# Causal scores of a two-attention kernel: from four stages of 128x32 array tiles to two stages of 32x32 array tiles

## The reference, cut to what matters

```python
hn = layernorm(x, ln1_w, ln1_b)
qkv = hn @ in_proj_w.T + in_proj_b
q, k, v = ...                        # (s=32, b=256, 16 heads, 8)
scores = jnp.einsum('sbnd,tbnd->bnst', q, k) / np.sqrt(HEAD_DIM)
scores = jnp.where(causal[None, None], scores, -jnp.inf)
probs = jax.nn.softmax(scores, axis=-1)
attn = jnp.einsum('bnst,tbnd->sbnd', probs, v).reshape(s, b, h)
attn = attn @ out_proj_w.T + out_proj_b
x1 = x + attn
hn2 = layernorm(x1, ln2_w, ln2_b)
... router, top 2 of 8, gates ...
hmid = jax.nn.gelu(jnp.einsum('th,ehf->tef', hn2, w1), approximate=False)
y = jnp.einsum('tef,efh->th', hmid * gates[:, :, None], w2)
return x1 + y
```

## Time and profile before

| what | value |
|---|---|
| time, median of 3 runs | 1313.66 us (1312.94 to 1315.72) |
| span of the profiled execution | 1312.0 us, mean granted PE clock 0.982 of full |
| PE / PEld busy | 1219.3 us (93%) / 783.7 us (60%) |
| DVE / ACT / POOL busy | 1059.6 us (81%) / 960.6 us (73%) / 312.5 us (24%) |
| chain that ended last, by engine | PE 62%, ACT 18%, issue 9%, DVE 8% |
| first phase | 0 to about 653 us |
| second phase | 653 to 1312 us, a step every 39.5 us |

### The profile page before, as it was taken

One profiled execution on the slowest core, in us unless ns is written; L12 is line 12 of the kernel. 1 busy time (PEld: TensorE's weight loads), 2 busy tenths in 40 slices (PEclk: granted clock), 3 DMA queues, 4 the chain that ended last, 5 costly groups with the idle time before them and its releaser, 6 DMA issues.

```text
span 1312.0 us, 35299 instructions
## 1 busy us (share of the span) xinstructions
PE 1219.3 (93%) x12100; PEld 783.7 (60%) x12100; DVE 1059.6 (81%) x3074; ACT 960.6 (73%) x1696; POOL 312.5 (24%) x510
## 2 busy tenths in 40 slices
PE   2699999999999999999768999999999999999998
PEld 1456666555656566565335666676666676666676
DVE  5888888888888888888457887888887888887873
ACT  1388898888888898888756667776667776667744
POOL 4334433343333433341120111110111110111000
PEclk9899999999999999999869999999999999999999
DMA  3000000000000000000010000000000000000000
GB/s 94 5 15 15 14 17 17 17 13 13 17 17 13 13 17 17 17 14 15 17 29 17 26 10 17 24 24 24 24 8 16 24 24 24 24 4 20 17 10 16
DMA packets 50855, 24.93 MB, mean 19 GB/s; under 512 B 6384, under 2 KB 50288, under 8 KB 50800
## 3 DMA queue, kind: packets, MB, share of 16 engines
q1 hardware_dynamic: 50800, 24.21, 6.6%
HBM read 15.28 MB, written 8.39 MB: 18 GB/s over the span
## 4 chain that ended last, share of the span: by engine, by line
PE 62%; ACT 18%; issue 9%; DVE 8%; ACTq 1%; DMA 1%; SPq 1%; POOL 1%; DVEq 0%; POOLq 0%
PE bank L515 54%; ACT Kexp L1353 6%; PE bank L546 4%; ACT hmid L1438 4%; ACT prob L1331 3%; DVE smax L1002 2%; PE bank L596 2%; ACT prob L1364 1%; DVE prob L1006 1%; ACT KT L1322 1%; PE bank L615 1%; DMA x_in<-in_L_attn_x 1%; ACT oT L1272 1%; ACT feat L1286 1%; DVE Vexp L994 1%
## 5 line engine op out<-in xcount | busy, mean ns | idle before, releaser
L924 DVE TENSOR_REDUCE rowmax<-bank 128x2 f32<-128x512 f32 x512 | 336.7, 685 | 59.5 <-PE bank L515 56.3
L1331 ACT ACTIVATE prob<-bank 128x512 f32<-128x512 f32 x512 | 294.0, 601 | 29.2 <-PE bank L515 24.6
L515 PEld LDWEIGHTS bank<-w_sb,hmid 128*128 128x128 f32 x2048 | 244.0, 192 | 23.7 <-issue 11.7
L1438 ACT ACTIVATE hmid<-bank,up_scale 128x512 f32<-128x512 f32 x256 | 176.2, 733 | 110.1 <-PE bank L515 109.9
L515 PE MATMUL bank<-w_sb,hmid 128*128 128x128 f32 x2048 | 248.2, 276 | 0.0
L1353 ACT ACTIVATE Kexp<-bank,head_bias,head_mask 128x512 f32<-128x512 f32 x256 | 188.2, 848 | 42.5 <-PE bank L515 42.5
L515 PE MATMUL bank<-QT,KT 128*128 128x256 bf16 x1024 | 197.3, 275 | 10.2 <-ACT prob L1331 7.1
L515 PE MATMUL bank<-KT,QT 128*128 128x256 bf16 x1024 | 200.4, 279 | 5.7 <-DVE rowmax L924 5.1
L1222 DVE SCALAR_TENSOR_TENSOR acc<-bank,gate,acc 128x128 f32<-128x128 f32 x512 | 143.3, 342 | 72.3 <-PE bank L515 70.2
L515 PE MATMUL bank<-prob,V 128*9 128x256 f32 x2048 | 159.6, 384 | 0.0
L1322 ACT COPY KT<-bank 64x1024 bf16<-64x1024 bf16 x128 | 128.8, 1007 | 27.6 <-PE bank L546 23.1
(11 more groups left out here) (164 smaller groups left out, 1846.6 us busy)
## 6 DMA issues: line engine op xcount, KB each, us to landing
x_in<-in_L_attn_x SPq DMA_DIRECT2D x32, 128.0 KB, 2.1
QT<-shiftT SPq DMA_DIRECT2D x256, 2.0 KB
z_scratch<-z_out SPq DMA_DIRECT2D x32, 128.0 KB, 1.8
xg<-in_L_attn_x SPq DMA_DIRECT2D x64, 64.0 KB, 1.9
zg<-z_scratch SPq DMA_DIRECT2D x64, 64.0 KB, 2.0
out<-acc SPq DMA_DIRECT2D x64, 64.0 KB, 1.7
w_sb<-in_L_ffn_w SPq DMA_DIRECT2D x1, 1024.0 KB, 6.8
in_wT<-in_L_ffn_in_proj_w SPq DMA_DIRECT2D x1, 192.0 KB, 2.4
```

Of the source, the lines that this page charges most:

```text
L515: return pe.matmul(o, l, r, start=start, stop=stop, skip_group_check=True)
L924: dve.tensor_reduce(rowmax[h // 8][:, :, h % 2, h % 8 // 2], row_scores[h % 3][:].rearrange("p (s t) -> p s t", s=ST), AX.X, ALU.max).then ...
L1331: act.activation(prob[:, h % 8].rearrange("p t s -> p (t s)"), col_scores[h % 2][:], ACT.Exp, scale=1.0 / D).then_inc(s_exp, 1)
L1438: act.activation(hmid[e % 2][c][:], up_bank[c][:], ACT.Gelu, scale=up_scale[:, 0:1]).then_inc(s_mid, 1)
```

## The change

It does five things.

1. `Kexp` holds four copies instead of sixteen. Copy j keeps in each block of 32 features (four heads) only head j of that block (`quad_mask`), so one block's rows of the four copies hold four heads. ACT issues 4 instead of 16 activations per group; each still writes 128 x 512.
2. The scores matmuls contract 32 features instead of 128, in the row block r of the array, with 128 columns instead of 512. A bank now holds four heads of all four token tiles, instead of all heads of one tile. There are 64 such matmuls per group where there were 16.
3. The four banks' worth of results are made in two stages k, each with both banks: two causal matmuls (now in different row blocks) and 32 small ones. Stage 1 waits for `s_sdiff >= 4n + 2`, that is, until DVE has finished both results of stage 0.
4. `causal` and `seq_eye` are copied by DVE to the other three blocks of 32 partitions once, in `prepare`.
5. The tables place the pieces anew: on PE v at u=8 (was 12) and the stages at u=10 and 12 (the four tiles were at 14, 14, 15, 15); on DVE v at 9 (was 11) and the maxima at 10, 11, 12, 13 (were all at 14).

```diff
-PE_G = dict(hn=0, q=2, k=4, v=12, pv=4, scores0=14, scores1=14, scores2=15, scores3=15, merge=6, out=9,
+PE_G = dict(hn=0, q=2, k=4, v=8, pv=4, scores0=10, scores1=12, merge=6, out=9,
...
-            def causal_scores(n, t):
-                if t < 2:
-                    if positive(2 * (n - 1) + t + 1):
-                        pe.wait_ge(s_son, 2 * (n - 1) + t + 1)
-                else:
-                    pe.wait_ge(s_sdiff, 4 * n + t - 1)
-                m = score_bank(n, t)
-                mm(m[:], seq_eye[:].rearrange("k n s -> k (n s)"), causal[:].rearrange("k h t -> k (h t)"),
-                   stop=False)
-                for q in range(QUAD):
-                    c = t * P + q * SEQ
-                    ins = mm(m[q * SEQ:(q + 1) * SEQ, :], gqT[:, c:c + SEQ],
-                             Kexp[:, t * QUAD + q].rearrange("p h t -> p (h t)"), start=False)
-                ins.then_inc(s_sc, 1)
+            def causal_scores(n, k):
+                if k == 0:
+                    pe.wait_ge(s_kexp, n + 1)
+                    if positive(2 * n):
+                        pe.wait_ge(s_son, 2 * n)
+                else:
+                    pe.wait_ge(s_sdiff, 4 * n + 2)
+                for r in (2 * k, 2 * k + 1):
+                    rows = slice(r * SEQ, (r + 1) * SEQ)
+                    mm(score_bank(n, r)[:], seq_eye[rows].rearrange("k q s -> k (q s)"),
+                       causal[rows].rearrange("k h t -> k (h t)"), stop=False)
+                for t in range(TILES):
+                    for q in range(QUAD):
+                        c = t * P + q * SEQ
+                        for r in (2 * k, 2 * k + 1):
+                            rows = slice(r * SEQ, (r + 1) * SEQ)
+                            ins = mm(score_bank(n, r)[q * SEQ:(q + 1) * SEQ, t * P:(t + 1) * P],
+                                     gqT[rows, c:c + SEQ],
+                                     Kexp[rows, t * QUAD + q].rearrange("p j t -> p (j t)"), start=False)
+                            if t == TILES - 1 and q == QUAD - 1:
+                                ins.then_inc(s_sc, 1)
...
+                for r in range(1, QUAD):
+                    dve.tensor_copy(causal[r * SEQ:(r + 1) * SEQ], causal[0:SEQ])
+                    dve.tensor_copy(seq_eye[r * SEQ:(r + 1) * SEQ], seq_eye[0:SEQ])
+                dve.tensor_reduce(quad_mask[:], head_mask[:].rearrange("p (r j) -> p j r", r=QUAD), AX.X,
+                                  ALU.add).then_inc(s_dve, 1)
...
-                for h in range(lo, hi):
-                    ins = act.activation(Kexp[:, :, h, :], head_bank(n)[:].rearrange("p (n t) -> p n t", n=GPOS),
-                                         ACT.Identity, bias=head_bias[:, h:h + 1], scale=head_mask[:, h:h + 1])
-                if hi == H:
+                ins = act.activation(Kexp[:, :, j, :], head_bank(n)[:].rearrange("p (n t) -> p n t", n=GPOS),
+                                     ACT.Identity, bias=head_bias[:, j:j + 1], scale=quad_mask[:, j:j + 1])
+                if j == QUAD - 1:
```

More of the change, by code:

```diff
@@ L210, in attention_and_experts_kernel @@
         head_mask = sb("head_mask", [P, H])
-        head_bias = sb("head_bias", [P, H])
-        seq_eye = sb("seq_eye", [SEQ, QUAD, SEQ], BF16)
-        causal = sb("causal", [SEQ, H, SEQ], BF16)
+        head_bias = sb("head_bias", [P, QUAD])
+        quad_mask = sb("quad_mask", [P, QUAD])
+        seq_eye = sb("seq_eye", [P, QUAD, SEQ], BF16)
+        causal = sb("causal", [P, H, SEQ], BF16)
         index8 = sb("index8", [P, TILES, NE])
@@ L464, in masks @@
                 pool.wait_ge(s_pool, own.next())
[L465 removed]
+                pool.memset(seq_eye[0:SEQ], 0.0).then_inc(s_pool, 1)
                 pool.wait_ge(s_pool, own.next())
[L467 removed]
+                pool.affine_select(out=seq_eye[0:SEQ], in_=seq_eye[0:SEQ], compare_op=ALU.not_equal, fill=1.0,
                                    base=0, pattern=[[0, QUAD], [-1, SEQ]], channel_multiplier=1).then_inc(s_pool, 1)
                 pool.wait_ge(s_pool, own.next())
[L470 removed]
+                pool.memset(causal[0:SEQ], 0.0).then_inc(s_pool, 1)
                 pool.wait_ge(s_pool, own.next())
[L472 removed]
+                pool.affine_select(out=causal[0:SEQ], in_=causal[0:SEQ], compare_op=ALU.is_ge, fill=MASKED,
                                    base=0, pattern=[[0, H], [-1, SEQ]], channel_multiplier=1).then_inc(s_pool, 1)
@@ L753, in first_head @@
                     causal_v(0)
-                for t in range(TILES):
-                    if slot == PE_FIRST[f"scores{t}"]:
-                        causal_scores(0, t)
+                for k in range(2):
+                    if slot == PE_FIRST[f"scores{k}"]:
+                        causal_scores(0, k)
             def prepare():
@@ L843, in group_step @@
                         causal_pv(g + 1)
-                    for t in range(TILES):
-                        if u == PE_G[f"scores{t}"] and head:
-                            causal_scores(g + 2, t)
+                    for k in range(2):
+                        if u == PE_G[f"scores{k}"] and head:
+                            causal_scores(g + 2, k)
                     if u == PE_G["merge"] and tail:
@@ L1077, in prepare @@
                 dve.tensor_copy(bv_wide[:], in_bT[:, 2:3].broadcast_to([P, P]))
-                dve.tensor_scalar(head_bias[:], head_mask[:], in_bT[:, 1:2], None, ALU.mult)
+                for r in range(1, QUAD):
[3 more added lines that the diff above has]
+                                  ALU.add).then_inc(s_dve, 1)
+                dve.wait_ge(s_dve, own.next())
+                dve.tensor_scalar(head_bias[:], quad_mask[:], in_bT[:, 1:2], None, ALU.mult)
                 dve.tensor_scalar(hn2_scale[:], ln2w[:], -1.0, None, ALU.mult)
@@ L1403, in first_head @@
                     hn_out(0)
-                for i in range(H // 2):
-                    if slot == ACT_FIRST["k0"] + i:
-                        expand_k(0, 2 * i, 2 * i + 2)
+                for j in range(QUAD):
+                    if slot == ACT_FIRST["k0"] + j:
+                        expand_k(0, j)
                 for t in range(TILES):
@@ L1452, in group_step @@
                         h2_out(g + 1)
-                    for i in range(H // 2):
-                        if u == ACT_G[f"k{i}"] and head:
-                            expand_k(g + 2, 2 * i, 2 * i + 2)
+                    for j in range(QUAD):
+                        if u == ACT_G[f"k{j}"] and head:
+                            expand_k(g + 2, j)
                 if tail:
```

19 lines of the change are left out of this document (10 added, 9 removed).

## The result

The changed kernel takes 1419.5 us (median of 4 runs, 1415.1 to 1420.0), the one before 1313.3 us (1312.4 to 1315.7). The ratio is 1.079, with a 95% interval of 1.078 to 1.081. The forecast was 1378 us, range 1350 to 1402: the sign was right, and the loss is 106 us where +64 was forecast. The profiled execution took 1419.2 us, its span is 1417.4.

A forecast was written before the change was run, and what follows sets the result against it. PE was taken to bound the second phase, ACT the last batch. 14 steps +65.8, step before them +3.9, setup +1.6, last batch -7: +64 us on the 1312.0 span, 1376; median run 1.7 higher: 1378 us, range 1350 to 1402.

The forecast's parts named there:

- Stage 1 waits for DVE: In each full step PE stands idle 5.3 us before stage 1 until DVE finishes stage 0's results; step +3.0 us.
- T: Start of `make_x1` on DVE in a step, from which the prediction measured everything in that step.
- DVE's wait for hn2T: DVE idle some 3 us before the split, behind stage 1, in a step.
- The stage: Scores on PE: a stage makes two results in 1.6 us at full clock, 2.8 at the low one.
- that rival: Row blocks don't overlap on PE: a stage is 2.6 us, cold 4.5; 1404 us, chance 0.12.
- A full-clock step: Full step of the second phase with PE at full clock: 42.5 us, +3.0.
- The clock: The idle gap brings PE to 1.2 GHz: stage 1 costs 2.8 instead of 1.6, transposes 0.5 more; step 44.2 us.
- PE's gain on the scores themselves: Scores on PE: two results in 1.6 us, not 2.64; frees 2.1 us per step by itself; issue not in the way.
- Setup: DVE's six copies and a reduction ahead of the scaling of the weights: +1.6 us (0.8 to 2.5).
- last batch: ACT bounds it; with 12 expansions fewer, PE is the next bound at about 9 us: -7 us (-4 to -9).
- The step g = -1: Step before the first full step: `make_x1` no earlier than 680.81, Exp at 700.7 against 696.78: +3.9 us.
- the first forecast: The whole sum, with the low clock behind the gaps: 1368 to 1390 us, chance 0.60.

The follow-up runs named there:

- Experiment 7: Changed kernel, stages at u=7 and 9, first maxima at u=6 ahead of the adds, V copies at u=7: 1295.9 us with group loop written out, 1325.2 with loop.
- experiment 4: Changed kernel with 24 unread f16 matmuls on PE ahead of stage 1: 1361.3 us, ratio 1.035.
- experiment 1: Kernel before with each scores matmul issued as four of 128 columns: 1430.7 us; repeated with the part as outermost loop: 1346.1 us.
- experiment 2: Changed kernel with the group loop written out: 1386.1 us; the same edit to the kernel before: 1314.5 us.
- experiment 3: Kernel before with each scores matmul in two or three parts, the part outermost, single runs: 1324.8 and 1326.6 us.
- experiment 6: Changed kernel, stages at u=7 and 9, first two maxima at u=7 behind an add: 1384.6 us with the loop, 1352.4 written out.
- experiment 5: Changed kernel with v and maxima put back to their old places, stages at u=14 and 15: 1362.3 us, ratio 1.036.

## Why the prediction was right in sign and too small in size

- **Stage 1 waits for DVE:** right. 12.49 us from T to stage 1 where 12.6 was forecast; a wait of 5.5 us in 13 of the 14 steps and 6.5 in the last (5.3 forecast); DVE's wait for hn2T behind it 4.54 us (I had said some 3). Experiment 7 shows the other half: with the same matmuls, and DVE's work put elsewhere, the wait is gone and the kernel gains.
- **The stage:** 1.40 us at full clock and 2.43 at the low one; forecast 1.6 and 2.8. Row blocks do overlap, and that rival is out.
- **A full-clock step:** 42.05 us in experiment 4; forecast 42.5.
- **The clock:** right in kind, too small. The row I used had 3.5 us of work at the low level, and I charged 1.7 us. Here it is nearly twice that: the first matmul back at full clock starts 7.2 us behind the wait (1108.28 to 1115.48), and experiment 4 measures 2.65. So the step is 44.7, not 44.2: 6.3 us over 14 steps, where the stage's and the step's better numbers are already taken off.
- **The step that failed: the loop's jump.** The prediction's "PE's gain on the scores themselves" counted the scores' instructions only to ask whether issue stands in the way of a stage. It left out what 384 more of them in the loop's body do to PE's fetching of its own code. This term was missing whole: five times 6.2 = 31 us. Experiments 1 and 2 show it from both sides. Neither the sum nor a rival had it, and the range ended 17 us short of the measured time. The Trainium skill, "Runtime: NRT & Kernel Launch" (Instruction fetch mechanics), says that a taken branch whose target is no longer held forces a fetch before execution goes on, and that written-out code is prefetched sequentially. The runs agree: 4.8 to 5.2 us idle at each jump in experiment 1, and in the written-out kernels no such row of gaps (single ones of 0.6 us in experiment 2, up to 1.4 in experiment 6 and 0.95 in experiment 7). The same section has TensorE hold 2048 instructions; by that 1654 matmuls and loads, about 1720 with the 71 waits, register and branch instructions that the trace records in the turn, would still have fitted, and experiment 3 shows that they were fetched again. The measurement decides.
- **Setup, last batch and the step before the first full one:** -1.5 us forecast, +2.3 measured. The setup was right. The first `rowmax` starts 2.8 us later than before (44.80 for 42.02), but from the second batch to the end of the first phase the distance is 1.6 to 1.7 us (1.6 forecast). Here are the same instruction near the end of the phase in the kernel before and in the changed one:

```profile
593.82 0.69 DVE L924 TENSOR_REDUCE rowmax<-bank 128x2 f32<-128x512 f32 x1 [0.70 <-PE bank L515]
```

```profile
595.52 0.69 DVE L934 TENSOR_REDUCE rowmax<-bank 128x2 f32<-128x512 f32 x1 [0.70 <-PE bank L516]
```

The last batch is what failed here: it gave back 2.2 us, not 7 (`z_out`, its last copy, ends it 0.6 us earlier than before, where it had started 1.7 later). The step g = -1 had its `make_x1` 2 us earlier than I allowed for, at 678.24, and then took 4.9 us more to the next one, not 3.9. At the end of the last batch PE is busy 14.44 us of 16 now:

```profile
636.00:652.00 16.00, 14.44 (x116) 6.14 (x122) 6.80 (x22) 10.33 (x19) 3.01 (x7) 0.87 0.04 11
...
656.72 0.39 PE L516 MATMUL bank<-causal,seq_eye 32*128 32x512 bf16 x2 [3.13 <-DVE prob L1016]
```

ACT had gone from 15.36 of 16 us to 10.33, as forecast, and then stage 1 waited for DVE here as well (3.13 us). How much of the missing 5 us is this wait and how much PE's own work isn't settled.

The miss in terms: 31 (jump) + 6.3 (clock) + 3.8 (the rest, most of it the last batch) = 41.1 us, against 105.4 - 64.3 = 41.1. In the first forecast's own range, 1368 to 1390, a kernel without the jump would have fallen: it measured 1386.

Left open: what sets the length of the idle time at a jump (1.6 to 5.3 us at 80 to 89 packets), and how much of the 6.2 us is fetch and how much clock in the changed kernel itself.

## What to carry to other kernels

Where a change splits matmuls inside a loop, count the loop's instructions on PE before and after, and look for idle time of PE without a releaser ("issue") at the jump; the packets of the instruction queue in the loop's stretch confirm it. If it is there, write the loop out or make the body smaller. Where work is cut into stages that share banks, the reader's time for one stage (here 2.73 us of DVE) has to be placed in a stretch in which the reader was idle, and its order must not put a wait for later work ahead of it. A gap costs its length and then the slow stretch behind it: here 2.65 us for 5.5.

## What the runs showed of the hardware

- The 32 small matmuls of a stage (64 in the trace, in f32) over two row blocks and four column blocks took 1.08 us (1098.44 to 1099.52): the blocks of rows do work beside each other.
- The four matmuls of 128 columns in a row into one column block made a result 2.40 us long (32 in the trace, experiment 1); the same ones, gone round over the four blocks, 1.0 us. The order alone makes the factor.
- A wait of 2.1 us was followed by the low clock in experiment 5, while idle times of 1.7 to 2.1 us in experiment 3 weren't (the matmul behind them took 0.39 us, and the granted clock from 800 to 1240 us is 1.00 in both runs). So the length of the gap alone doesn't decide it. In experiment 6 a wait of 1.68 us was followed by full clock for the stage, and by a granted clock of 0.50 in the window 1064 to 1067:

```profile
1064.00:1067.00 3.00, 3.00 (x16) 3.00 (x15) 1.99 (x10) 0.00 (x0) 0.00 (x0) 0.50 0.00 0
```
